# Splitting the natural-order contexts once, in layer 1, and loading the parts in both attentions of layer 3

## The reference, cut to what matters

```python
# the end of layer 1
x = x + y * g @ Wo.T
xc = ln(x); sxc = shifted(xc) - xc
rr = sigmoid((xc + sxc * fmaa_r) @ fWr.T)
kk = square(relu((xc + sxc * fmaa_k) @ fWk.T))
x = x + rr * (kk @ fWv.T)
# layer 3, twice (i = 1, 2); kv = ctx_2048
h = ln(x); qh = h @ wq + bq
kh = concat(kv @ wk + bk, bias_k); vh = concat(kv @ wv + bv, bias_v)
x = x + (softmax(qh . kh / sqrt(128)) . vh) @ wo + bo
```

## Time and profile before

| | us |
|---|---|
| median of 3 runs (2767.01 to 2772.35) | 2772.2 |
| the profiled execution, its own time | 2768.3 |
| its span, first to last instruction | 2766.5 |
| TensorE busy in the span | 2494.0 (90%) |
| VectorE, ScalarE, GpSimd busy | 1396.1, 1139.6, 1117.7 |
| mean granted TensorE clock | 0.946 of full speed |

### The profile page before, as it was taken

The page is one execution under the profiler, slowest core; times in us unless marked ns, Lnnn a source line. Parts: engine busy times, 40 slices in busy tenths (PEclk is TensorE's granted clock), DMA queues, the critical chain, the costliest instruction groups (busy, mean ns, idle before and its releaser), DMA issues. The chain is left out here.

```text
span 2766.5 us, 37822 instructions
## 1 busy us (share of the span) xinstructions
PE 2494.0 (90%) x14008; PEld 2181.9 (79%) x14008; DVE 1396.1 (50%) x2343; ACT 1139.6 (41%) x2439; POOL 1117.7 (40%) x498
## 2 busy tenths in 40 slices
PE   7888479989998788899979999998998999999698
PEld 5666334578984456599879999988997899999698
DVE  4666621388884432233345666633333565664643
ACT  3777121223322311123455666632235565665321
POOL 2100322342212110262277878836224887876300
PEclk9999669999998899899989999999999999999899
DMA  7453601699972015143754545415275544542300
GB/s 232 115 124 76 213 13 52 183 248 240 236 183 83 0 61 172 57 165 132 266 174 131 161 144 169 153 46 199 102 254 171 168 144 142 163 142 94 112 31 24
DMA packets 215850, 385.68 MB, mean 139 GB/s; under 512 B 88740, under 2 KB 127676, under 8 KB 215028
## 3 DMA queue, kind: packets, MB, share of 16 engines
q1 hardware_dynamic: 215668, 383.28, 44.8%
HBM read 288.03 MB, written 103.35 MB: 141 GB/s over the span
## 5 line engine op out<-in xcount | busy, mean ns | idle before, releaser
L1777 PE MATMUL att_ring<-ca_pp,att_arena 128*128 128x400 f32 (+1 forms) x2304 | 439.3, 349 | 27.4 <-POOL att_arena L1859 15.5
L1777 PEld LDWEIGHTS att_ring<-ca_pp,att_arena 128*128 128x128 f32 (+1 forms) x2304 | 423.7, 192 | 36.7 <-POOL att_arena L1859 20.2
L1848 POOL TENSOR_TENSOR att_arena<-att_arena 128x1448 fp32r<-128x1448 f32 x64 | 212.2, 3315 | 255.4 <-ACT att_arena L1865 255.4
L1777 PE MATMUL att_ring<-att_arena,qk_wh 128*128 128x362 f32 x1024 | 257.4, 333 | 0.0
L2461 DVE TENSOR_TENSOR ca_yl<-att_ring,att_arena 128x400 fp32r<-128x400 f32 x256 | 146.6, 573 | 203.7 <-ACT att_arena L2420 203.7
L1859 POOL TENSOR_TENSOR att_arena<-state_X,att_arena 128x1536 fp32r<-128x1536 f32 x64 | 224.4, 3507 | 5.0
L1856 POOL TENSOR_TENSOR att_arena<-state_X,att_nothing 128x1536 fp32r<-128x1536 f32 x64 | 176.1, 2751 | 47.0 <-DMA state_X<-in_ctx 47.0
L1777 PE MATMUL att_ring<-att_arena,qk_wl 128*128 128x362 f32 x512 | 173.8, 339 | 18.8 <-POOL att_arena L2042 18.4
L1777 PEld LDWEIGHTS att_ring<-att_arena,qk_wh 128*128 128x128 f32 x1024 | 186.6, 193 | 0.0
L2420 ACT ACTIVATE att_arena<-att_ring 128x400 fp32r<-128x400 f32 x256 | 128.8, 503 | 95.0 <-PE att_ring L1777 94.8
L1871 ACT ACTIVATE att_kstage<-att_score,att_shift 100x362 f32<-100x362 f32 x256 | 143.8, 563 | 44.5 <-DVE att_shift L1884 44.4
(11 more groups left out here) (403 smaller groups left out, 6028.7 us busy)
## 6 DMA issues: line engine op xcount, KB each, us to landing
att_arena<-keys SPq DMA_DIRECT2D x64, 724.0 KB, 5.2
state_X<-in_ctx SPq DMA_DIRECT2D x64, 512.0 KB, 3.8
queries<-att_arena SPq DMA_DIRECT2D x16, 1600.0 KB
att_arena<-queries SPq DMA_DIRECT2D x64, 400.0 KB, 3.9
keys<-rec_stage SPq DMA_DIRECT2D x32, 724.0 KB, 4.4
keys<-att_kstage SPq DMA_DIRECT2D x32, 724.0 KB, 3.5
l_arena<-kept_value SPq DMA_DIRECT2D x176, 100.0 KB, 6.1
state_X<-in_ctx SPq DMA_DIRECT2D x64, 210.0 KB, 4.2
```

What stands on the lines that cost most here:

```text
L1777: issued = nc.tensor.matmul(out, x, y, start=(first and k == 0), stop=(last and k == count - 1))
L1848: self.nc.gpsimd.tensor_tensor(self.kl[:, n % 2].bitcast(F32R), self.kl[:, n % 2], self.kh[:, n % 2].bitcast(F32), ALU.subtract).then_inc( ...
```

## The change

The split of the context, made 64 times before (8 batches, four groups, two attentions), is made 8 times, in layer 1. A class `ContextParts` does it in the four product blocks: batches 0 and 1 in `l1z`, 2 and 3 in `l1g`, 4 to 6 in `l1h`, 7 in `l1i`. SyncE loads a batch (two DMAs) into one of two buffers in the gate's tile, ScalarE rounds it (two instructions), GpSimd subtracts (two instructions), SyncE stores both parts in DRAM (four DMAs). In layer 3 SyncE loads the parts, two DMAs of twice the bytes, straight into the double buffer that `mix` reads; the wait for `x_ready` is gone, the load of step n+1 waits for `mix(n-1)`, and `mix(n)` waits for the DMA. `split_context` is gone. `load_context(0)` stands ahead of a wait for `rows_out`. In layer 0 the memset of the spare rows and the wait for it are gone, and the small tile `tmp` of layer 1 lies in `z`.

```diff
+class ContextParts:
+        flat = gate.rearrange("p b c l -> p (b c l)")
+        self.raw = [flat[:, i * 3 * C:(i + 1) * 3 * C].rearrange("p (t c) -> p t c", c=C) for i in range(2)]
+        self.high = [ahead.fwh[:, 0:3], sc.sb("part_high", [P, 3, C], F32R)[:]]
+        self.low = [ahead.fwl[:, 0:3].bitcast(F32R), sc.sb("part_low", [P, 3, C], F32R)[:]]
...
+    def load(self, sp, b):
+        if b >= 2:
+            sp.wait_ge(self.low_done, 2 * (b - 1))
+        sp.dma_start(self.raw[b % 2][:, 0:2], ...).then_inc(self.raw_in[b % 2], 16)
+        sp.dma_start(self.raw[b % 2][0:self.row, 2], ...).then_inc(self.raw_in[b % 2], 16)
+    def round(self, act, b):
+        act.wait_ge(self.raw_in[b % 2], 32 * (b // 2 + 1))
+        if b >= 2:
+            act.wait_ge(self.kept[b % 2], 64 * (b // 2))
+        self.nc.scalar.activation(self.high[b % 2][:, 0:2], self.raw[b % 2][:, 0:2], ACT.Copy).then_inc(self.high_done, 1)
...
+    def subtract(self, pool, b):
+        pool.wait_ge(self.high_done, 2 * (b + 1))
+        self.nc.gpsimd.tensor_tensor(self.low[b % 2][:, 0:2], self.raw[b % 2][:, 0:2], self.high[b % 2][:, 0:2].bitcast(F32),
+                                     ALU.subtract).then_inc(self.low_done, 1)
...
+    def store(self, sp, b):
+        sp.wait_ge(self.low_done, 2 * (b + 1))
+        for k, part in enumerate((self.high, self.low)):
+            sp.dma_start(self.out[b, :, k, 0:2], part[b % 2][:, 0:2].bitcast(F32)).then_inc(self.kept[b % 2], 16)
+            sp.dma_start(self.out[b, 0:self.row, k, 2], part[b % 2][0:self.row, 2].bitcast(F32)).then_inc(self.kept[b % 2], 16)
+    def finish(self, sp):
+        for i in range(2):
+            sp.wait_ge(self.kept[i], 64 * (B // 2))
@@ layer 1
+            def opening(sp):
+                parts.load(sp, 0)
+                parts.load(sp, 1)
+                for b in range(2):
+                    parts.store(sp, b)
+                    parts.load(sp, b + 2)
+            def passing(first, end):
+                def moves(sp):
+                    for b in range(first, end):
+                        parts.store(sp, b)
+                        if b + 2 < B:
+                            parts.load(sp, b + 2)
+                    if end == B:
+                        parts.finish(sp)
@@ product_transposed (l1h, batches 4, 5, 6), ScalarE, after the relu of bank u
+                    if name == "scalar" and u - 2 in range(len(batches)):
+                        parts.round(other, batches[u - 2])
@@ product_rows (l1z 0, 1; l1g 2, 3; l1i 7), GpSimd
                 nc.gpsimd.tensor_tensor(sl[:, b % RING_S], ...)
+                if b == 5 and batches:
+                    parts.subtract(pool, batches[0])
+            for k in batches[1:]:
+                parts.subtract(pool, k)
@@ product_rows, ScalarE
                     high_source(b + RING_S)
+                if b in (2, 4) and b // 2 - 1 < len(batches):
+                    parts.round(act, batches[b // 2 - 1])
@@ layer 3
     def load_context(self, sp, n):
-        sp.wait_ge(self.x_ready, n)
-        sp.dma_start(self.craw[:, 0:2, :], self.ctx[b, 0:2 * P, :]...).then_inc(self.x_in, 16)
-        sp.dma_start(self.craw[0:STILES[2][1], 2, :], self.ctx[b, 2 * P:S, :]).then_inc(self.x_in, 16)
+        if n >= 2:
+            sp.wait_ge(self.y_full, CC * (n - 1))
+        sp.dma_start(self.x[:, n % 2, :, 0:2].bitcast(F32), self.ctx_parts[b, :, :, 0:2]).then_inc(self.x_in[n % 2], 16)
+        sp.dma_start(self.x[0:rows, n % 2, :, 2].bitcast(F32), self.ctx_parts[b, 0:rows, :, 2]).then_inc(self.x_in[n % 2], 16)
-    def split_context(self, pool, n):
...
                 if k == 1:
+                    t.load_context(sp, 0)
                     sp.wait_ge(t.rows_out, 16)
-                    t.load_context(sp, 0)
...
-                if n + 1 < STEPS:
-                    t.split_context(pool, n + 1)
...
             def mix(n):
-                pe.wait_ge(x_ready, n + 1)
+                pe.wait_ge(x_in[n % 2], 32 * (n // 2 + 1))
```

More of the change, by code:

```diff
@@ L187, with grouped_attention @@
 KROWS = 2 * SLOTS * D0
-def grouped_attention(nc, a, X, spare, ident, columns, column, qh, ql, Wk, Wv, bv, heads_of, ctx, outT, late, last_out, queries, keys,
+def grouped_attention(nc, a, X, ident, columns, column, qh, ql, Wk, Wv, bv, heads_of, ctx, outT, late, last_out, queries, keys,
                       row_sums, inverses):
@@ L1404, in rwkv_layer @@
             stats, added = st.sb("stats", [L, B, 6]), st.sem("added")
-            product_rows(nc, "l1z", W["WoT"], z, add_and_sum(X, stats, added))
+            a["ctx_parts"] = nc.dram_tensor("ctx_parts", (B, P, 2, 3, C), F32).ap()
+            parts = ContextParts(nc, st, ahead, gate[:], a["ctx"], a["ctx_parts"])
+            def opening(sp):
[12 more added lines that the diff above has]
+                        parts.finish(sp)
+                return moves
+            product_rows(nc, "l1z", W["WoT"], z, add_and_sum(X, stats, added), parts=parts, batches=(0, 1), moves=opening)
             await_copies(nc, (last, 3))
@@ L1427, in square_positive @@
                     nc.vector.tensor_tensor(part, part, part, ALU.mult)
-            product_transposed(nc, "l1h", W["fWkT"], sq, keep_positive, engines=("scalar",), behind=square_positive)
+            product_transposed(nc, "l1h", W["fWkT"], sq, keep_positive, engines=("scalar",), behind=square_positive, parts=parts,
+                               batches=(4, 5, 6), moves=passing(4, 7))
             gated = st.sem("gated")
@@ L1435, in add_gated @@
                 e.tensor_tensor(X[:, b, :], X[:, b, :], tmp[:, b % 2, :], ALU.add)
-            product_rows(nc, "l1i", W["fWvT"], dev, add_gated)
+            product_rows(nc, "l1i", W["fWvT"], dev, add_gated, parts=parts, batches=(7,), moves=passing(7, B))
 def clear(nc, t):
@@ L1480, in product_transposed @@
+def product_transposed(nc, prefix, weight, source, store, engines=("scalar", "vector"), tiles=CC, behind=None, parts=None, batches=(),
+                       moves=None):
     with Scope(nc, prefix) as sc:
@@ L1498, in keep, with _ @@
                     store(engine, n, half, banks[u][:, :, 0:L])
-        if aside:
+                    if name == "scalar" and u - 2 in range(len(batches)):
+                        parts.round(other, batches[u - 2])
+        if parts:
             @block.gpsimd
             def _(pool):
-                aside()
+                for b in batches:
+                    parts.subtract(pool, b)
+            @block.sync
+            def _(sp):
+                moves(sp)
         @block.scalar
@@ L1513, in _, with product_rows @@
                 behind(dve)
-def product_rows(nc, prefix, weight, source, store, engine_name="vector", aside=None, arrived=()):
+def product_rows(nc, prefix, weight, source, store, engine_name="vector", aside=None, arrived=(), parts=None, batches=(), moves=None):
     RING_S = 3
@@ L1782, with __init__ @@
 class Heads:
-    def __init__(self, nc, sc, spare, ident, ctx, queries, keys, rows):
-        self.nc, self.ctx, self.queries, self.keys, self.rows, self.ident = nc, ctx, queries, keys, rows, ident
+    def __init__(self, nc, sc, spare, ident, ctx_parts, queries, keys, rows):
+        self.nc, self.ctx_parts, self.queries, self.keys, self.rows, self.ident = nc, ctx_parts, queries, keys, rows, ident
         self.arena = sc.sb("arena", [P, 2 * B * CC * SP], F32R)
@@ L2760, in attention_block @@
     with Scope(nc, f"att{i}") as outer:
-        t = Heads(nc, outer, spare, ident, a["ctx"], queries, a[f"keys{i}"], rows)
+        t = Heads(nc, outer, spare, ident, a["ctx_parts"], queries, a[f"keys{i}"], rows)
         projections(nc, f"qk{i}", t, X, a["ctxT"], weights, a[f"head_columns{i}"], a[f"bo{i}_rows"], a[f"value_rows{i}"], scratch,
@@ L2780, in program @@
         a["filled"] = nc.alloc_semaphore("filled")
[L2781 removed]
+        gqa_layer(nc, a, X, ident, columns, column)
         clear_semaphores(nc)
```

66 lines of the change are left out of this document (32 added, 34 removed).

## The result

The changed kernel took 2759.78 us (median of 7, 2756.34 to 2761.95) against 2771.15 for the kernel before (median of 7, 2767.01 to 2773.03): a ratio of 0.9966, interval [0.9954, 0.9977], 11.4 us faster by the medians and 9.4 by the ratio. On the chip of the second group of experiments it was 0.9987 [0.9977, 0.9997], 3.1 us by the medians. The forecast was 2752, so the time lies inside its range and on its side, but the gain is well under the forecast one: 20 us against the median before, 17.0 by the prediction's own sum. The profiled span went from 2766.5 to 2757.6 us.

The account below looks back on a forecast made before the run. GpSimd's context split was taken to bound the attention starts, TensorE the rest. The terms: -27.1 + 2.0 - 2.0 + 3.9 + 4.3 + 1.9 = -17.0 us, from 2768.3 to 2751.3, stated as 2752; range 2739 to 2766.

Parts of the forecast that it names:

- the two added costs: Layer 1: 4.3 us in `l1h` plus 1.9 for the start of `l1i`; projections: 3.9 us over both attentions.
- What bounded the attention starts: First four steps of each attention: GpSimd's context split delays `mix(1)` to `mix(3)`; removing it gains 13.0 and 14.1 us.
- the named steps: `mix(1)`, `mix(2)` and `mix(3)` at each attention's start, where TensorE waits for the low part of the context.
- Late next is ScalarE: Attention starts: ScalarE, waiting for step 6's keys, holds `mix(3)`'s evictions; charged 1.0 us per attention, 2.0 in all.
- Steady gaps: Steady attention steps: two gaps of "issue", 3.1 us from 1450 to 1850; gain 1.0 us per attention, 2.0.
- more gain: Rival, 2742, chance 0.15: with GpSimd idle VectorE's L1884 is short, ScalarE runs ahead, steady gaps and half the charges go.
- Projections: the term: Where queries are made: `load_context(0)`'s extra 0.74 MB makes query weights 1.9 us later; 3.9 us in both attentions.
- `l1h`: the term that failed: Layer 1's third block: ScalarE waits for batch 6's load behind four stores, landing at 968.9; 4.3 us longer.
- `l1z`, `l1g`, `l1i` at nothing: Layer 1's other blocks: the added rounding and subtraction fit in; cost nothing, up to 2 us in all.
- the cold start of `l1i`: Start of `l1i`: after 8 us of wait TensorE's first batch runs slower; 1.9 us, ends 0 to 2.5.
- Half the gain: Rival, 2765, chance 0.20: ScalarE and the DMA queue take over GpSimd's hold; only the named 13.6 us go.
- Slower: Rival, 2782, chance 0.10: small copies land late behind longer context loads, so ScalarE and TensorE stand in every attention step.

Follow-up runs that it names:

- the second group of experiments: The changed kernel run again, unchanged, on the chip of the next three runs: 2762.29 us against 2765.42 for the kernel before, ratio 0.9987.
- load_first: Against the changed kernel, each layer 1 load issued ahead of the stores of the batch whose buffer it takes: 2760.92 us, ratio 0.9985 to the kernel before.
- 0.9903: Against the changed kernel: two batches per block, each block's last load after it, first context load behind the third key load; 2738.52 us, ratio to the kernel before.

## Why the prediction fell short

Two terms failed, and not the mechanism of the gain. The attentions came as forecast, 27.0 us, and the two added costs were 13.5 us more than charged, 14.3 for 6.2 in layer 1 and 9.3 for 3.9 in the projections.

**What bounded the attention starts, and that term: right.** GpSimd's order was the chain of every one of the named steps. Forecast for the first four steps, with the charge of 1.0 each: -12.0 and -13.1. From the start of `mix(0)` to the end of `mix(3)` they went, by the means of four traces with before's contexts and five of the change, from 51.7 to 41.4 and from 53.4 to 40.2 us: -10.3 and -13.3. In this pair of traces it was 52.0 to 42.7 and 55.0 to 39.7, -9.3 and -15.3; 1.9 us of the second stood ahead of `mix(1)`, beyond the wait of 0.70 that the prediction had removed there. That the total over both attentions met the forecast within 0.1 us is partly luck: 1.5 us less came in the first four steps, and 1.4 more behind them.

**Late next is ScalarE: right, and dearer in one attention.** I charged 1.0 us each. In the first, in this trace, ScalarE waited 1.80 us for `ca_extra` and 1.57 for the keys, TensorE 2.04, and `mix(3)` ran 1.5 us longer: 3.5. In the second it was 0.70 us. Counted from `mix(0)`, the copies of step 2 went out 7.8 us earlier than before (26.8 us behind it instead of 34.6), where I had put some 9.

**Steady gaps: wrong in the first place named.** Two waits of "issue", 3.0 us from 1464 to 1848, where the earlier trace rows has 3.1. They weren't the context splits'. The kernel before had other waits in that stretch (1450 to 1850), which the earlier trace rows leaves out and which are gone:

```profile
PE att_ring L1777 <- POOL att_arena L1859: 1.4, 2, 1.1
PE att_ring L2535 <- DVE ca_yl L2461: 1.4, 1, 1.4
```

So the 2.0 us came, 2.3 and 1.1 behind the fourth step by the means, but not out of the gaps that were named. VectorE's line of the earlier trace rows after:

```profile
L1955 DVE SCALAR_TENSOR_TENSOR att_shift<-att_top,att_zeros x64: 161/2073/2284, 1367.6 to 2518.5; 100x4 f32<-100x4 f32 x64
```

Its median stays at 2073 ns: the keys, all that GpSimd still does in a step (3.3 us), still hold it: it takes 0.16 us in the 11 of 64 cases where no GpSimd instruction runs beside it. So "more gain" had the right rule, and the keys alone are enough to keep it in force.

**Projections: the term mis-sized, 9.3 for 3.9.** The weights were later by about the bytes' time, but I counted the delay and not the clock behind it: 181 matmuls at 0.89 instead of 0.96, 2.9 us in the first projections.

**`l1h`: the term that failed, 9.6 for 4.3.** The chain was the right one and the wait was named. Its sizes weren't. The load landed 2.6 us later than forecast: 0.8 because SyncE's five issues ahead took longer, 1.8 because it took 6.3 us and not the 4.5 of the earlier trace rows, a row of another stage without 1.48 MB of stores just ahead. What follows took 2.0 us more, and 1.0 of that is a slip of the sum: from a landing at 968.9, a rounding of 1.6 us ends at 970.5, not at 969.5, so by its own numbers the term was 5.3. I also took the load as the only condition. The store is one too. In the change it was met 3.8 us before the load and cost nothing by itself, but load_first shows that it takes over as soon as the load comes first.

**`l1z`, `l1g`, `l1i` at nothing: 3.0 in `l1g`**, 0.5 and 1.2 in the others (with the cold start of `l1i` charged apart at 1.9, which is more than all that `l1i` lost). I had seen that SyncE's issues end with the block and wrote 2 as the upper end for all. Without the stores `l1g` takes 25.6 us, and with them but with the last load behind the block 25.0: it is the last load's place behind the stores that the block paid for.

**The rivals.** "Half the gain", 2765, was nearer to both measurements' gains than the forecast was, but on another path: the full 27 us came, and 24 were to be paid elsewhere. "Slower" needed a wait for the small copies in every step; there is one of 1.8 us in the first attention's start and one of 0.5 in the second's.

## What to carry to other kernels

Where a moved pass runs through two buffers, ask of each turn what must have left the buffer as well as what must have come in, and price both by the bytes that are in the DMA engines at that time. Spread such turns so that each lies a block away from the one it reuses, and keep issues that nobody awaits out of a block whose end waits for the queue: here that was 14.6 of the 23.8 us between 0.9987 and 0.9903, with the same work. A load placed first in a queue is paid by whatever is behind it, and by the lower clock after the gap: 8.9 us in the two projections here.

## What was not expected of the hardware

SyncE's issues can lengthen in a burst: the store of 210 KB (L1530) takes 0.43 us as the second issue at 962.08, 0.89 as the fourth, and 1.64 at 968.12, as the tenth. The number of issues ahead is not the whole of it, since the eighth, at 966.52, took 0.44; what sets it is not shown. Six DRAM to DRAM transfers, 11.8 MB together, took 44.07 us to issue. A wait on two semaphores shows one releaser: with the load named it was 9.94 us, and taking that load ahead of the stores made it 8.92 us with a store named.
